# Attention stage: q's parts stored once and loaded in nine pieces, parts stored ahead of the first half's maxima

## The reference, cut to what matters

```python
q = _rope(q, positions); k = _rope(k, positions)
scores = jnp.einsum('bhqd,bhkd->bhqk', q, k) / jnp.sqrt(jnp.float32(dk))
scores = jnp.where(causal[None, None, :, :], scores, -jnp.inf)
attn = jax.nn.softmax(scores, axis=-1)
out = jnp.einsum('bhqk,bhkd->bhqd', attn, v)
```

## Time and profile before

| | us |
|---|---|
| median of three runs | 2100.93 |
| the profiled execution | 2113.99 |
| its span, first to last instruction | 2112.1 |
| attention, start-up (about 1313 to 1382) | 69 |
| attention, eight turns (about 1382 to 1840) | 458 |
| TensorE busy in the whole span | 1749.1 |
| VectorE busy | 1430.3 |

### The profile page before, as it was taken

One profiled execution on the slowest core, in us unless ns is written; L12 is line 12 of the kernel. 1 busy time (PEld: TensorE's weight loads), 2 busy tenths in 40 slices (PEclk: granted clock), 3 DMA queues, 4 the chain that ended last, 5 costly groups with the idle time before them and its releaser, 6 DMA issues. The chain is left out here.

```text
span 2112.1 us, 22867 instructions
## 1 busy us (share of the span) xinstructions
PE 1749.1 (83%) x7317; PEld 859.9 (41%) x7317; DVE 1430.3 (68%) x1594; ACT 991.5 (47%) x1553; POOL 908.9 (43%) x507
## 2 busy tenths in 40 slices
PE   7788888888898888887773946698888889888998
PEld 5233333333333333332363834244444445543333
DVE  3099999999999999999661113466566566374444
ACT  3566656656666666655221423144444455441211
POOL 1277777777878777777533142211111110040000
PEclk8899999999999999999976976589999999988999
DMA  3111221221221212212003320503323320100001
GB/s 136 41 61 61 80 80 60 80 80 60 80 80 60 80 60 80 80 60 81 36 19 93 96 62 14 150 2 77 77 78 77 78 77 3 45 0 0 0 0 40
DMA packets 49067, 128.07 MB, mean 61 GB/s; under 512 B 5478, under 2 KB 36046, under 8 KB 39094
## 3 DMA queue, kind: packets, MB, share of 16 engines
q1 hardware_dynamic: 45782, 117.65, 17.4%
q0 software_dynamic: 3216, 9.51, 1.3%
HBM read 104.04 MB, written 23.01 MB: 60 GB/s over the span
## 5 line engine op out<-in xcount | busy, mean ns | idle before, releaser
L535 POOL TENSOR_TENSOR PR<-H,CS 128x1024 f32<-128x1024 f32 x256 | 602.1, 2357 | 193.0 <-DVE H L510 184.1
L510 DVE TENSOR_TENSOR_SCAN H<-DA,X 128x1024 f32<-128x1024 f32 x256 | 583.6, 2280 | 4.1 <-ACT DA L496 4.1
L433 PE MATMUL psY<-PR,W 128*128 128x512 f32 x1024 | 500.0, 612 | 1.1 <-POOL PR L535 1.1
L496 ACT ACTIVATE DA<-DT,negA 128x511 f32<-128x511 f32 x512 | 332.0, 711 | 82.1 <-DVE H L510 81.7
L503 DVE TENSOR_TENSOR X<-DU,psB 128x1024 f32<-128x1024 f32 x256 | 314.5, 1228 | 63.7 <-POOL DU L554 36.6
L433 PEld LDWEIGHTS psY<-PR,W 128*128 128x128 f32 x1024 | 198.4, 196 | 245.0 <-issue 238.7
L1222 ACT ACTIVATE a_PT<-a_psS 128x512 f32<-128x512 f32 x320 | 181.4, 601 | 138.4 <-PE a_psS L1126 134.4
L1269 DVE TENSOR_REDUCE a_MX<-a_psM 128x1 f32<-128x384 f32 (+3 forms) x352 | 205.0, 636 | 47.1 <-PE a_psM L1141 45.7
L413 PE MATMUL psB<-ST,sel 96*128 96x512 bf16 x256 | 101.7, 397 | 109.5 <-DVE X L503 109.4
L1140 PE MATMUL a_psM<-a_kst,a_qst 72*128 72x512 bf16 (+3 forms) x512 | 147.1, 335 | 27.8 <-DMA a_kst<-scratch_k 17.2
L1125 PE MATMUL a_psS<-a_qst,a_kst 75*128 75x512 bf16 (+3 forms) x512 | 135.7, 313 | 1.4 <-ACT a_PT L1222 0.4
(11 more groups left out here) (252 smaller groups left out, 2523.0 us busy)
## 6 DMA issues: line engine op xcount, KB each, us to landing
CS<-c_rows SPq DMA_DIRECT2D x64, 1024.0 KB, 4.7
scratch_q<-a_partsq SPq DMA_DIRECT2D x24, 384.0 KB, 3.6
a_qst<-scratch_q SPq DMA_DIRECT2D x8, 1152.0 KB
a_kst<-scratch_k SPq DMA_DIRECT2D x24, 384.0 KB
scratch_k<-a_partsk SPq DMA_DIRECT2D x8, 384.0 KB, 4.4
slots<-zeros POOLq DMA_DIRECT2D x1, 2624.0 KB, 10.1
stok<-slots SPq DMA_DIRECT2D x3, 768.0 KB, 7.1
work<-in_pack SPq DMA_DIRECT2D x1, 2272.0 KB, 8.1
```

The costliest lines, as they stand in the source:

```text
L433: last = nc.tensor.matmul(chunk(psY, c), w("ident"), chunk(PR[n % 4], c), start=False, stop=n == NS - 1)
L496: last = nc.scalar.activation(DA[:, s % 4, c, 1:T], chunk(DT[p], c)[:, 1:T], ACT.Exp, scale=negA[:, c * NS + s:c * NS + s + 1])
L510: nc.vector.tensor_tensor_scan(H[s % 4][:, :], DA[:, s % 4, :, :].rearrange("p c t -> p (c t)"), X[s % 2][:, :], 0.0, ALU.mult, ALU.add).t ...
L535: nc.gpsimd.tensor_tensor(both(PR[s % 4][:, :]), both(H[s % 4][:, :]), CS[q % 2][:, s % 4, :].unsqueeze(1).to_broadcast([P, NCH, T]), ALU. ...
```

## The change

`store_parts` stores q's parts once instead of three times, into copy 0 of `scratch_q`. `load_stack` fills `qst` with nine DMAs of 8 rows (8 x 16 KB = 128 KB each) instead of one of 72 rows: for each part three DMAs read the same 8 rows of `scratch_q`. `kst` is loaded as before. The counts in the semaphores follow (two stores for a block, twelve loads). In SyncE's turn `store_parts` moves ahead of `send_maxima` of the first half.

```diff
-        LOADS = 4 * 16
+        LOADS = 12 * 16
@@
-                    act.wait_ge(parts_stored, 64 * b)
+                    act.wait_ge(parts_stored, 32 * b)
@@
-            for c in range(3):
-                sp.dma_start(scratch_q[pb, :, c].rearrange("a p t -> p a t"), parts[0][:, :, :]).then_inc(parts_stored, 16)
+            sp.dma_start(scratch_q[pb, :, 0].rearrange("a p t -> p a t"), parts[0][:, :, :]).then_inc(parts_stored, 16)
             sp.dma_start(scratch_k[pb].rearrange("c p t -> p c t"), parts[1][:, :, :]).then_inc(parts_stored, 16)
 
         def load_stack(sp, b, pb):
-            sp.wait_ge(parts_stored, 64 * b + 64)
-            sp.dma_start(qst[pb][0:MROW, :], scratch_q[pb].rearrange("a c (j h) t -> (a c j) (h t)", h=HEADS)).then_inc(st_loaded[pb], 16)
+            sp.wait_ge(parts_stored, 32 * b + 32)
+            for a in range(3):
+                for c in range(3):
+                    at = 24 * a + 8 * c
+                    sp.dma_start(qst[pb][at:at + 8, :], scratch_q[pb, a, 0].rearrange("(j h) t -> j (h t)", h=HEADS)).then_inc(st_loaded[pb], 16)
             for a in range(3):
                 sp.dma_start(kst[pb][24 * a:24 * a + 24, :],
@@
                     if c.more_m:
+                        if c.more_p:
+                            store_parts(sp, c.t + 2, c.p)
                         send_maxima(sp, c.t + 1, 0, c.base + c.use["MA"] + 1, 1 - c.p)
                         if c.more_p:
-                            store_parts(sp, c.t + 2, c.p)
                             sp.wait_ge(S_ready, UNITS_T * c.t + UNITS_T + 1)
                             load_stack(sp, c.t + 2, c.p)
```

## The result

The changed kernel takes 2165.4 us (median of four runs, 2163.3 to 2172.5) against 2101.9 for the kernel before on the same terms: ratio 1.0304, 95% interval 1.0278 to 1.0329, 63.5 us more. I had forecast 2195 (+94) in a range of 2100 to 2212. The direction holds, and so does the wait through which the loss comes; the forecast size was half as large again as what came.

What follows compares the result with a forecast made beforehand. TensorE's slot 2 wait on the stack loads bounds the kernel. Six turns, each load 16.0 us longer but 3.6 earlier, give +74, the start-up +20: 2101 + 94 = 2195 us, range 2100 to 2212.

Steps and rivals of the forecast that it cites:

- What bounds the kernel: Attention turns: TensorE sets the pace, waiting in slot 2 for the stack loads, six stalls of 25.1 us together.
- Step 1: Stores of a block: two q stores fewer, 0.79 MB instead of 1.57, 2.3 us less and two issues less.
- Step 2: SyncE's turn: load issued when slot 8 begins, 3.6 us earlier per turn; maxima held at most 2 us, taken as nothing.
- Step 3: qst load: nine issues take 3.7 us instead of 0.31, hidden behind the transfers.
- Step 4: qst load: 8-row DMAs at 52 GB/s, q taking 22.5 us, 16.0 more per load; bounds were 181 GB/s and 52.
- The reason behind that rate: Stack loads: only the number of rows of a DMA sets rates apart, 181 GB/s for 72 rows, 157 for 24.
- The start-up: Block 0: its load 16 us longer, stores 2.3 shorter; first scores at about 1402.5 instead of 1382.05, +20 us.
- The clock: Turns: no further term, since clock already falls to 0.5 in the stall; without the stall 2.6 us per turn return.
- rival A: Stack loads: queued pieces add up, load keeps 16.5 us, starts 3.6 us earlier, 2062 us; chance 0.13.
- B: Stack loads: eight DMA engines at 13 GB/s each, +3.8 us per load, 2104 us; chance 0.10.
- C: q load: neighbouring pieces overlap in pairs, 105 GB/s, +4.8 us, 2112 us; chance 0.14 with what lies up to the forecast.
- The signs: Profile: load issue within 0.3 us of slot 8's start, slot 2 stall 15 to 17, maxima landing over 25.

Runs made afterwards that it cites:

- order-only kernel: Kernel before with only the stores moved ahead of the first half's maxima, three q stores and one 72-row load kept: 2095.3 us, ratio 0.9950.
- doubled kernel: Changed kernel with kst too loaded in nine pieces of 8 neighbouring rows: 2224.2 us, ratio 1.0580.

## Why the prediction came out as it did

- **What bounds the kernel** (the loop through slot 8, load, slot 2): right. In the changed kernel the load ends 8.3 to 8.5 us later and a turn is 7.7 longer; with hardly any load left a turn is 7.0 shorter, the stall and what I put down to the clock; engine work is the same to 2%.
- **Step 1, two stores fewer:** right. In the start-up the q and k stores take 3.7 us from first issue to the load's issue instead of 6.0, the 2.3 forecast.
- **Step 2, the order:** right in the main: 1.44 us from issue to landing against 1.39, with 2.2 and 2.5 in two turns. TensorE's matmuls waited 0.8 us for them in all the turns and its weight loads 1.6, where it was nothing and 0.5. The load starts 3.6 us earlier by SyncE's waits, 3.8 by its mean distance from slot 8's first exponential. Without step 1 it would have cost 2.4 us per turn, as the order-only kernel shows; the 2 us a turn that I had named as the most was for two stores, not four.
- **Step 3, nine issues:** right; 2.97 us for nine, behind the transfers. With the rows apart an issue costs 0.64 us, and then it is as long as the transfer of the piece.
- **Step 4, the rate of an 8-row piece:** the right end of the bounds, and the term that was mis-sized. I took 52 GB/s, from "24 rows at 157 make 8 rows at 52". Where pieces of neighbours run by themselves they make 66 GB/s or more, and in the changed kernel the stretch behind the first piece, in which `kst` rows are moved beside them, makes 85. The load grew by 12.1 us and not by 16.0. With 12.1 in place of 16.0 the sum for the turns is 6 x (12.1 - 3.6) = 51; the stalls grew by 50.5, the turns by 47.3. I had also laid `kst` behind `qst`, at 157 GB/s, where in truth the two overlap and the tail runs at 96. At 66 GB/s for q and 157 for k my sum would give 17.9 + 7.5 + 2.5 = 27.9 us, near the measured 28.8, but it would be right by errors that cancel.
- **The reason behind that rate:** I had taken "the number of rows of a DMA". The runs say otherwise. The row count is not the cause: eight rows nine apart run at 186 GB/s, eight neighbours at 66, and 24 rows gain when they are spread. That a rule on the row count gave the right direction was luck: with neighbouring rows, fewer rows also means fewer groups of partitions. The time for one row is 0.61 us with rows nine apart, 1.04 to 1.23 two apart and 2.06 side by side. The Trainium skill, page SBUF — State Buffer, section "Door 1: The DMA port swizzle", gives a cause, four neighbouring partitions on one port; the order of the loads in these runs agrees (16 to 17 us with no sharing, 24 with two rows on a port, 35 on average with four, both stacks in pieces). Its 27.2 GB/s per port is too low for this case: four rows of 16 KB in 2.06 us are 32 GB/s, if by that page four share a port. What width such a group has was not measured by itself; these runs would fit a wider one too.
- **The start-up:** the step is right and its size again too large, +12.8 instead of +20, for the same reason. The small maxima store did wait behind block 1's load, 14.6 us, and TensorE waited for it (2.03 us).
- **The clock:** nearly right for the changed kernel (the work at the low clock behind the stall takes about 1.4 us less, which I had at nothing; at half its cost that gives back 0.7 us a turn, near the 3 us by which the turns grew less than the stalls), and right for rival A: the clock stays up when the stall goes, and 2.8 us per turn come back beside the stall, against my 2.6. That these 2.8 are the clock's was not tried by itself.
- **The rivals:** A (pieces add up) did not come, but rows nine apart produce it on purpose, at 2067 to 2071 us where I had worked out 2062. B (eight engines at 13 GB/s each) fails: the same eight-row pieces move 186 GB/s. C (105 GB/s) lies near the 97 GB/s of the shortest load of the doubled kernel.
- **The signs:** the load's issue beside slot 8's first exponential came, and so did a load over 20 us. Three came too small, all by the mis-sized rate: the stall in slot 2 (11.1 to 13.7 us for 15 to 17), the landing of the second half's maxima (19.4 to 21.9 us after their issue for over 25) and the start-up.

## What to carry to other kernels

How fast a DMA of few rows fills SBUF depends on where the rows land, and not only on how many bytes or rows it has: here eight 16 KB rows in neighbouring partitions cost nearly three times what they cost nine partitions apart (66 against 186 GB/s). If a tile's row order is free, as a contraction's is, interleave the pieces; it is a change of an index, and done for both stacks it took the changed kernel from 3% slower than the kernel before to 1.7 and 1.9% faster. And before a small transfer that a fast engine needs is queued behind large stores, count what these hold it up: here 2.4 us per turn with 1.57 MB ahead, and with 0.79 MB at most 0.4.

## What the runs showed of the hardware that I had not expected

- A DMA whose SBUF rows are two, three or nine partitions apart takes SyncE 0.6 to 0.85 us to issue; with neighbouring rows it is mostly 0.33 to 0.5 (once 0.73, in the order-only kernel).
- Of a piece's eight rows each takes 0.61 us nine partitions apart, about 1.1 two apart and 2.06 side by side.
- The same queue of eighteen neighbour pieces runs at 66 or at 97 GB/s from one turn to the next; at 66 its rows start eight at a time, about 2.06 us apart.
